# Centring by a matrix product in a transformer layer's normalisation: ScalarE reads the bank, VectorE's subtraction goes

## What is computed

```python
def ffn_layer(x, g, bln, W1, b1, W2, b2):
    mu = x.mean(-1, keepdims=True)
    var = ((x - mu) ** 2).mean(-1, keepdims=True)
    xn = (x - mu) / jnp.sqrt(var + 1e-05) * g + bln
    hg = xn @ W1 + b1
    a, gate = jnp.split(hg, 2, -1)
    return a * jax.nn.gelu(gate, approximate=False) @ W2 + b2
for i in range(DEPTH):
    x = attn_layer(shift_tokens(x), Wqkv[i], q_scale[i], k_scale[i], Wo[i]) + x
    x = ffn_layer(shift_tokens(x), ln_g[i], ln_b[i], W1[i], b1[i], W2[i], b2[i]) + x
```

## Time and profile before

| | |
|---|---|
| median of 3 runs | 4436.79 us (4434.71 to 4437.3) |
| span of the profiled execution | 4434.3 us (the page gives no other time of this execution) |
| PE busy | 4165.1 us, 94% |
| DVE busy | 3726.7 us, 84% |
| ACT busy | 3248.1 us, 73% |
| POOL busy | 1784.9 us, 40% |
| feature phase, layers phase, experts | to about 523 us, to about 3880 us, to the end |

### The profile page before, as it was taken

The page is one execution under the profiler, slowest core; times in us unless marked ns, Lnnn a source line. Parts: engine busy times, 40 slices in busy tenths (PEclk is TensorE's granted clock), DMA queues, the critical chain, the costliest instruction groups (busy, mean ns, idle before and its releaser), DMA issues. The chain is left out here.

```text
span 4434.3 us, 116364 instructions
## 1 busy us (share of the span) xinstructions
PE 4165.1 (94%) x43493; PEld 3282.5 (74%) x43493; DVE 3726.7 (84%) x6488; ACT 3248.1 (73%) x5137; POOL 1784.9 (40%) x965
## 2 busy tenths in 40 slices
PE   6888589999999999999999999999999999979999
PEld 2444268887888878888788887888878888747776
DVE  7888788888888888888888888888888888667776
ACT  5888567777777777777777777777777777646666
POOL 0000165554555555555555555555545555200000
PEclk9999899999999999999999999999999999989999
DMA  2111133332332323323233232332323332211110
GB/s 84 44 44 41 38 70 69 67 71 61 89 71 66 71 62 88 72 64 71 62 88 73 63 71 62 88 74 64 69 62 94 68 70 63 56 62 46 48 43 29
DMA packets 351688, 287.85 MB, mean 65 GB/s; under 512 B 231920, under 2 KB 236400, under 8 KB 350000
## 3 DMA queue, kind: packets, MB, share of 16 engines
q1 hardware_dynamic: 351152, 280.60, 26.1%
HBM read 45.45 MB, written 4.33 MB: 11 GB/s over the span
## 5 line engine op out<-in xcount | busy, mean ns | idle before, releaser
L681 POOL TENSOR_TENSOR qk_rotated<-qk_rotated,rotary_sines 128x1024 f32<-128x1024 f32 x384 | 924.8, 2408 | 1496.0 <-DVE rotary_sines L763 1496.0
L692 POOL TENSOR_TENSOR qk_rotated<-qk_rotated,rnorm 128x1024 f32<-128x1024 f32 x384 | 733.8, 1911 | 7.4
L771 DVE TENSOR_REDUCE qk_sumsq<-qk_squared 128x16 f32<-128x1024 f32 x384 | 465.1, 1211 | 92.0 <-ACT qk_squared L518 92.0
L232 PE MATMUL ps_proj<-qkv_w_hi,x_shifted_hi 128*128 128x512 f32 x1152 | 512.2, 445 | 18.4 <-DVE rotary_sines L763 11.6
L525 ACT ACTIVATE q_t<-ps_qk_t 128x512 f32<-128x512 f32 x384 | 229.7, 598 | 406.8 <-PE ps_qk_t L288 398.1
L753 DVE TENSOR_TENSOR qk_rotated<-ps_proj,rotary_scaled 128x1024 f32<-128x1024 f32 x384 | 466.9, 1216 | 4.5 <-ACT qk_squared L518 4.2
L763 DVE TENSOR_TENSOR rotary_sines<-ps_proj,rotary_scaled 128x1024 f32<-128x1024 f32 x384 | 466.0, 1213 | 1.4 <-POOL qk_rotated L681 1.4
L234 PE MATMUL ps_proj<-qkv_w_hi,x_shifted_lo 128*128 128x512 f32 x1152 | 459.7, 399 | 0.0
L539 ACT ACTIVATE k_t_by_head<-ps_qk_t 64x512 f32<-64x512 f32 x768 | 451.0, 587 | 10.5 <-PE ps_qk_t L297 1.1
L233 PE MATMUL ps_proj<-qkv_w_lo,x_shifted_hi 128*128 128x512 f32 x1152 | 455.8, 396 | 0.0
L313 PE MATMUL ps_scores<-k_t_by_head,q_t 128*32 128x128 f32 x12288 | 415.1, 276 | 10.0 <-issue 4.8
(11 more groups left out here) (304 smaller groups left out, 9687.8 us busy)
## 6 DMA issues: line engine op xcount, KB each, us to landing
v_by_window<-v_tokens SPq DMA_DIRECT2D x1152, 128.0 KB, 2.4
v_by_window<-v_tokens SPq DMA_DIRECT2D x384, 64.0 KB, 2.0
k_t_by_head<-k_t_by_head SPq DMA_DIRECT2D x96, 256.0 KB, 4.3
e_w_in<-combine_saved SPq DMA_DIRECT2D x64, 256.0 KB, 3.1
v_by_window<-v_by_window SPq DMA_DIRECT2D x192, 64.0 KB, 2.0
qkv_w_raw<-in_layer_qk_dram SPq DMA_DIRECT2D x7, 1664.0 KB, 8.8
f_k_stacked<-f_k_hi SPq DMA_DIRECT2D x64, 64.0 KB, 2.0
f_k_stacked<-f_k_lo SPq DMA_DIRECT2D x64, 64.0 KB, 2.0
```

The costliest lines, as they stand in the source:

```text
L232: mm(out, hi, HI[:, o:o + 512], start=True, stop=False)
L681: tt(u, u, TB[:], ALU.add).then_inc(added, 1)
L692: tt(u, u, r.unsqueeze(3).broadcast_to((P, 2, 8, DH)), ALU.mult).then_inc(scaled, 1)
L771: nc.vector.reduce_sum(SS[:, 16 * i:16 * i + 16], SQ[:].rearrange("p (h e) -> p h e", e=DH), AX).then_inc(sumsq, 1)
```

## The change

PE's product uses a new constant, CENTER, which is the identity less 1/128 everywhere, so that the bank holds the centred stream and not the mean. ScalarE squares it from the bank into ZQ and copies it from the bank into ZC. VectorE's `center` and the semaphore `centered` are gone; `normalize` waits for `z_sq`, which the copy now raises. ScalarE waits for the product (`mean_mm`), for the previous use of DG (`bc_mm`) and for the previous use of ZC (`normed`). CENTER is built once by VectorE.

```diff
+        CENTER = sb("centering", [P, P])
...
-        NSETUP = 9
+        NSETUP = 10
...
-                    mm(X[:, 0:N], MEAN[:], ZS[:], start=True, stop=True).then_inc(mean_mm, 1)
+                    mm(X[:, 0:N], CENTER[:], ZS[:], start=True, stop=True).then_inc(mean_mm, 1)
...
-                    act.wait_ge(centered, m.n + 1)
-                    a(ZQ[:].rearrange("p t k -> p (t k)"), ZC[:], ACT.Square).then_inc(z_sq, 1)
+                    act.wait_ge(mean_mm, m.n + 1)
+                    after(act, bc_mm, m.n)
+                    a(ZQ[:].rearrange("p t k -> p (t k)"), X[:, 0:N], ACT.Square)
+                    after(act, normed, m.n)
+                    a(ZC[:], X[:, 0:N], ACT.Copy).then_inc(z_sq, 1)
...
-            def center(m):
-
-                if m.live:
-                    dve.wait_ge(mean_mm, m.n + 1)
-                    dve.wait_ge(zs_built, m.n * 2 + 2)
-                    tt(ZC[:], ZS[:], X[:, 0:N], ALU.subtract).then_inc(centered, 1)
-
...
-                    dve.wait_ge(centered, m.n + 1)
+                    dve.wait_ge(z_sq, m.n + 1)
...
-                center(e)
...
+            ts(CENTER[:], IDENT[:], -1.0 / D, None, ALU.add).then_inc(setup, 1)
```

More of the change, by code:

```diff
@@ L126, in layers_phase @@
         v_out, v2_in = sem("v_out"), sem("v2_in")
-        wo_half, wo_mm, resid1, zs_built, mean_mm, centered, z_sq, var_mm = (sem(x) for x in (
-            "wo_half", "wo_mm", "resid1", "zs_built", "mean_mm", "centered", "z_sq", "var_mm"))
+        wo_half, wo_mm, resid1, zs_built, mean_mm, z_sq, var_mm = (sem(x) for x in (
+            "wo_half", "wo_mm", "resid1", "zs_built", "mean_mm", "z_sq", "var_mm"))
         diag, bc_mm, normed, affine, w1_mm, gated, hid, w2_mm, resid2 = (sem(x) for x in (
```

## The result

The changed kernel takes 4470.16 us (median of 4 runs, 4465.64 to 4474.01) against 4436.85 us (median of 4 runs, 4434.71 to 4437.3): ratio 1.0075, 95% interval 1.0063 to 1.0088. It is slower by 33.3 us, as forecast in sign; the forecast was 25.6 us. The time lies 8 us above the predicted 4462 and inside the range, 4447 to 4483.

A forecast was written before the change was run, and what follows sets the result against it. PE was taken to bound the kernel, without room, so that ScalarE's delays lengthen the turn: 94 x 0.27 = 25.4 us plus 0.2 for setup, 25.6 on the median 4436.79, gives 4462, range 4447 to 4483.

The forecast's parts named there:

- The mask's delay: ScalarE's mask behind the Copy: 0.28 us later, less 0.09 slack, so the scores 0.19 later by it.
- VectorE's saving: VectorE's queue loses the subtraction, 0.33 us in each of 96 turns, which turns into idle time: worth 0.
- ScalarE's price, first half: ScalarE's queue: Square and Copy take 0.29 to 0.42 us each, so the stretch grows 0.26 to 0.52, taken as 0.28.
- The delay of q's copy: ScalarE brings q's copy 0.28 us later to k's transposes (L297), where PE already waited: PE 0.28 later.
- The slack at the scores: Between the mask's end and PE's scores: 0.09 us, after a step of about 0.04 from ScalarE to PE.
- Variance's delay: PE's variance products wait for the Copy: 0.26 us less 0.03 slack, so they start 0.23 later.
- What is given back at the gate products: PE's waits for VectorE's gate products (L232, L420) shift by 0.23 only; turn grows 0.23 to 0.28, taken as 0.27.
- The number of turns: Layers phase: 94 turns grow, 82 waiting at L297 and 10 with weight divisions; 94 x 0.27 = 25.4 us.
- A: Rival: VectorE sets the turn and ScalarE has room; faster by 0.33 us in 96 turns, 4405; 7%.
- B: Rival: PE has unseen slack or gives the delay back; growth below 0.09 us a turn, 4437 to 4446; 10%.
- C: Rival: ScalarE's two instructions don't overlap with what follows; growth 0.49 us a turn, 46 in all, 4483; 15%.
- The 0.29 per turn: ScalarE's stretch by the skill page's instruction cost (306 ns for 256 elements): grows 0.29 us, 94 turns give 27 us.

The follow-up runs named there:

- e4: Kernel before, VectorE's subtraction kept, plus one more ScalarE Copy of 128x256 from ps_tail into a spare tile behind the Square: 4471.56 us, ratio 1.0078.
- e3: Changed kernel with the Copy into ZC moved from ScalarE to VectorE, in the subtraction's place: 4444.06 us, ratio 1.0017.
- e8: Kernel before with the mask ahead of the Square, variance behind pv (products with v) and variance_arg behind norm_out: 4426.61 us, ratio 0.9983.
- e11: Changed kernel, but VectorE instead of ScalarE copies the bank into ZC and squares, with one operand in the bank: 4437.07 us, ratio 1.0000.
- e2: Changed kernel, Copy still ahead of the mask, but the Square alone releases the variance, whose products go to bank ps_qk_t: 4468.76 us, ratio 1.0071.
- e1: Changed kernel with ScalarE's Copy behind the mask; the Square alone releases the variance, its products in bank ps_qk_t: 4443.89 us, ratio 1.0017.
- e12: e11 with the variance behind pv and variance_arg behind norm_out: 4416.26 us, ratio 0.9958.

## Why the prediction was right, and where its sizes were off

It was right in sign and in the cause, ScalarE's queue ahead of the mask. It was right in size partly by luck: the waits that it made up its 0.27 us from, the variance's (0.23) and q's copy's (0.28), are not what lengthens the turn. The mask's delay does, which it had as the smallest of the three (0.19).

- **VectorE's saving is worth 0**: right. e4 keeps the subtraction and takes the same time; the wait before variance_arg grew to 1.44, forecast 1.4.
- **ScalarE's price, first half**: Square and Copy out of the bank last 385 and 378 ns, forecast 385, and Square to Copy is 0.28, forecast 0.29: right. Copy to mask was mis-sized: 0.40 in place of 0.29. The row taken for it (L584 to L548) overlaps by 0.10, the pair of the changed kernel doesn't. e3 shows the 0.10 by itself. The range's upper end had it (0.42).
- **The delay of q's copy** was 0.27 to 0.28 as forecast (4.97 to 5.24 at k's transposes), because L564 behind the mask made up the other 0.09. But it didn't set the turn: q's copy at 4.60 with the 1.04 of e8 from there to k's projection gives 5.64, an estimate, 0.09 later than before and not 0.28.
- **The slack at the scores** is the step that failed. I took 0.09 us, from a step of 0.04 between ScalarE's end and PE's load at L297. Here the scores start 0.13 after the mask's end before (2221.86 to 2221.99) and also in the changed kernel (1889.02 to 1889.15), where they do wait: the slack was 0. e11 agrees: there the mask ends 0.31 earlier, and the scores, held by the variance alone, start less than 0.01 earlier. So the mask's 0.36 (0.28 + 0.40 - 0.32) and the 0.02 by which it lasts longer came through whole: 0.38 a turn, not 0.27.
- **Variance's delay**: right in its size (its weight load waits 0.20 us in 92 turns, forecast 0.2 to 0.3), but it doesn't count: e2 removes it and nothing changes, since the mask holds the scores longer.
- **What is given back at the gate products**: nothing. I thought they would shift by less; they follow pv, which follows the scores, and so carry the whole delay.
- **The number of turns**: 94 was too many. 77 plain turns and four of 36.5 to 36.8 us grew; of the turns about a division of weights five are 35.3 us long in both kernels, and the five longest scatter (42.4 to 42.7 before, 42.2 to 43.1 after), where 0.23 each had been forecast. 81 x 0.38 = 30.8, measured 30.7 between the first and the last Square, against 94 x 0.27 = 25.4: two errors that partly cancel.
- **Rivals**: A (VectorE sets the turn) is refuted by e4, B (PE's slack) by the turn itself, C (no overlap at all, 0.49) was right about one of the two joints, the Copy and the mask. The 0.29 per turn by the Trainium skill, page "ScalarE: Activation LUTs", section "What ACT_TABLE_LOAD costs", went wrong by the same joint and the same slack as my 0.28. The trace agrees with its overlap from Square to Copy (0.11 in the rows above) and not from Copy to mask (0.02 of idle time).

What stays open is why the mask doesn't overlap with the instruction ahead of it in the changed kernel, e1, e2 and e3. It overlapped with one that reads SBUF, and with k's copies out of another bank, as in another slot of the changed kernel's turn:

```profile
1870.01 1.20 ACT L540 ACTIVATE k_t_by_head<-ps_qk_t 64x512 f32<-64x512 f32 x2
1871.11 0.58 ACT L549 ACTIVATE ps_scores<-mask 128x512 f32<-128x512 f32 x1
```

There it starts 0.10 before the end. That the bank ps_tail is read ahead of it isn't enough to explain it: in e4 the mask stands behind a Copy of 128x256 out of the same bank and starts 0.10 before its end.

```profile
2023.44 0.38 ACT L586 ACTIVATE spare<-ps_tail 128x256 f32<-128x256 f32 x1
2023.72 0.60 ACT L549 ACTIVATE ps_scores<-mask 128x512 f32<-128x512 f32 x1
```

There the Copy has another target and a Square out of SBUF ahead of it; no run varied these two by themselves.

## What to carry to other kernels

On an engine with idle time an instruction is not free if a short one that another engine is waiting for stands behind it: look at what follows in the queue, not at the busy share. Where two engines meet with no wait in the profile, measure the step from end to start at that very pair before calling the remainder slack: it was 0.13 us from the mask to the scores and 0.05 from q's copy to k's transposes (medians). And the wait that the profile names (variance's, q's copy's) need not be the one that sets the turn: e2 took one away and nothing moved; e8 moved pv, and the wait that went was that of k's projection, behind four instructions of VectorE.

## What the runs showed of the hardware

A VectorE product of 128x256 with both operands in SBUF took 2354 ns in the median while GpSimd ran a TENSOR_TENSOR on SBUF, and 425 at the least; the same product with one operand in PSUM took 421 in the same place. The Trainium skill, page "Perfetto Trace Analysis", section "Optimizing Scalar/DVE Operations", says that GpSimd and VectorE share a read port of SBUF; the trace agrees, and here it is VectorE that is held up: its product ends 0.28 us after GpSimd's instruction. The product with an operand in PSUM ran beside the same GpSimd instruction in 93 of 96 turns of e11 and was not held up. Here this is what centring by PE gives: it leaves the centred values in PSUM, so that VectorE can square them beside GpSimd, and with the variance behind pv that is the fastest order tried (e12, 0.42% below the kernel before, interval 0.26 to 0.59%; e8, which centres on VectorE, 0.17%). Whether VectorE could square out of SBUF in a place where GpSimd is idle was not tried.
